# Another order of work in a local attention, and a quarter of a scan's product handed to GpSimd

## The chip, the cores and the metric

One NeuronCore of one Trainium2 chip runs the whole program. Its engines each run their own queue of instructions in order: TensorE (PE, with its weight loads as PEld), VectorE (DVE), ScalarE (ACT), GpSimd (POOL), and SyncE (SP), which here only issues DMAs. They meet through semaphores. The metric is device time in microseconds; a kernel's time is the median of its runs.

## The reference, cut to what matters

The reference is a stack of blocks on a residual of 4 sequences x 1024 tokens x 128 features in float32. The change touches two of them. The first is the selective scan, used once with 64 channels and 32 states and once with 256 channels and 16 states:

```python
def step(h, inputs):
    u_t, d_t, b_t, c_t = inputs
    dA = jnp.exp(d_t[..., None] * A)
    h = dA * h + (d_t * u_t)[..., None] * b_t[:, None, :]
    y = jnp.einsum('bdn,bn->bd', h, c_t)
    return (h, y)
```

The second is local attention with 8 heads of 64 features and windows of 64 tokens, each looking at its own window and the one before; it runs in four layers (two stages of depth 2):

```python
h = shift_token(x); qkv = h @ wqkv; q, k, v = jnp.split(qkv, 3, axis=-1)
q = l2norm(q) * qs; k = l2norm(k) * ksc
q, k = rotary_xpos(q, k)
sim = jnp.einsum('bhwid,bhwjd->bhwij', bq, bk)          # bq is q times 8, bk: own window and the one before
sim = jnp.where(mask, -jnp.finfo(sim.dtype).max, sim)
out = jnp.einsum('bhwij,bhwjd->bhwid', jax.nn.softmax(sim, axis=-1), bv)
x = x + out.reshape(b, n, INNER) @ wo
```

## The kernel before

The program is eight stages, one after the other. Within a stage each engine has its own hand-written order of calls inside a `Block`; a call begins with its waits and ends with the increment of a semaphore. `s.at(n)` is the value after n increments, so `pe.wait_ge(q_in.sem, q_in.at(i + 1))` waits for the copy of Q of tile i.

**The scan** (`scan`) takes 16 steps j for each run of one sequence (and half of the channels): 4 runs in stage 1 and 8 in stage 7, 192 steps. A step covers 128 partitions x 1024 time columns. ScalarE makes the decay in PSUM (L233), GpSimd the input product (L249) from rows of B that SP fetched, VectorE the scan (L258), TensorE spreads C over the partitions (`spread_c`, L207, PSUM banks 2 and 3, a single buffer), VectorE multiplies state by C (L273), and TensorE folds the product into banks 6 and 7 (L221). At the end of a run VectorE takes the sum (`take`, L264).

**Local attention** (`local_attention`) takes 32 tiles of 128 tokens in a layer, software-pipelined by `in_steps`: 4 tiles written out, a loop over groups of 4, the last tiles written out. The names, with their lines in the trace:

- SP: `fetch(i + 4)` brings the token-shifted input of a tile to its place with four DMAs (L1605 to L1608); `pair_values(i + 1)` waits for V of the tile (L1612) and copies its halves with two DMAs (L1614, L1615). In each step SP does `fetch(i + 4)`, then `pair_values(i + 1)`.
- TensorE: `scores` (L1674), `values` (L1691), `output` (L1708), `project_qk` (L1640), `project_v` (L1645), `turn_probs` (L1681), `turn_qk` (L1652), `masks` (L1660), `turn_in` (L1634), `turn_out` (L1700), in this order in a step.
- ScalarE: `exponential` (L1775), `square` (L1757), `copy_probs` (L1780), `copy_k` (L1770, L1771), `take_v` (L1764), `copy_out` (L1785), `copy_h` (L1752).
- VectorE: `maximum` (L1845), `subtract` (L1851), `normal` (L1857, L1860), `add` (L1866), `squares` (L1836), `rotate` (L1827, then L1829 and L1830), `copy_q` (L1841).
- GpSimd: `norm`, four instructions a tile (L1902, L1904, L1907, L1911).

`turn_in` and `output` share bank 7; `turn_qk`, `values` and `turn_out` share banks 5 and 6; scores, mask and turned probabilities share banks 3 and 4.

Of the kernel before, what the change touches and what calls it, by code (L numbers as in the profile page):

```python
# [14 lines left out]
P = 128  # L15
# [130 lines left out]
def scan(k, batches, halves_n, delta, du, parts, rows, stored, sel, a_col, fold, diag, u, out, gate, spare):  # L146
# [4 lines left out]
    c_up, decay_up, input_up, scanned, weighted, summed, y_taken = [  # L151
        k.count("scan_" + n) for n in ("c_up", "decay_up", "input_up", "scanned", "weighted", "summed", "y_taken")]
    lane_in = [k.count(f"scan_lane_in{s}") for s in range(U)]
    credited = (input_up, scanned, weighted, summed, y_taken)
    for s in credited:
        s.passed(U)
    runs = [(b, hf) for b in range(batches) for hf in range(halves_n)]
    with ExitStack() as mem:
        b_lane = k.arena[4].rearrange("p (s t) -> p s t", t=SEQ)
        ring2 = k.arena6.rearrange("p (r s t) -> p r s t", r=3, t=SEQ)  # L160
        inputs, weight = ring2[:, 0], ring2[:, 2]
        state = [ring2[:, 1, 0], ring2[:, 1, 1]] + spare
        bank = k.bank
        pieces = len(rows(0, 0))
        block = mem.enter_context(nc.Block())
# [7 lines left out]
        def ahead(o, j, n):  # L173

            if isinstance(j, int) and j + n >= J:
                return (o + 1, j + n - J) if o + 1 < len(runs) else None
            return o, j + n

        def steps(eng, body, begin=None):

            for o in range(len(runs)):
                if begin:
                    begin(o)
                with eng.Fori(0, J // U - 2) as jj:
                    for s in range(U):
                        body(o, jj * U + s, s)
                for j in range(J - 2 * U, J):
                    body(o, j, j % U)
# [13 lines left out]
        @block.tensor  # L202
        def _(pe):
            def spread_c(o, j):
                pe.wait_ge(weighted.sem, weighted.at(o * J + j))
                for c in range(2):
                    mm = pe.matmul(bank[2 + c], sel(j), parts(runs[o][0], c), start=True, stop=True)  # L207
                mm.then_inc(c_up.sem, 1)

            def begin(o):  # L210
                b, hf = runs[o]
                pe.wait_ge(y_taken.sem, y_taken.at(o))
                for c in range(2):
                    pe.matmul(bank[6 + c][0:M, :], diag(hf), u(b, hf, c), start=True, stop=False, skip_group_check=True)

            def body(o, j, s):
                pe.wait_ge(weighted.sem, weighted.at(o * J + j + 1))
                if ahead(o, j, 1):
                    spread_c(*ahead(o, j, 1))
                for c in range(2):  # L220
                    mm = pe.matmul(bank[6 + c][0:M, :], fold, weight[:, s % 2, c * BANK:(c + 1) * BANK], start=False,  # L221
                                   stop=isinstance(j, int) and j == J - 1, skip_group_check=True)
                mm.then_inc(summed.sem, 1)

            spread_c(0, 0)
            steps(pe, body, begin)

        @block.scalar
        def _(act):
            def decay_of(o, j, s):  # L230
                b, hf = runs[o]
                act.wait_ge(scanned.sem, scanned.at(o * J + j - 1))
                act.activation(decay(s), delta(b, hf), ACT.Exp, scale=a_col(hf, j)).then_inc(decay_up.sem, 1)  # L233

            def body(o, j, s):
                if ahead(o, j, 2):
                    decay_of(*ahead(o, j, 2), s)

            for j in range(2):
                decay_of(0, j, j)  # L240
            steps(act, body)

        @block.gpsimd
        def _(pool):
            def body(o, j, s):
                i = o * J + j
                pool.wait_ge(lane_in[s % U].sem, lane_in[s % U].at((i - s % U + U) * (16 * pieces // U)))
                pool.wait_ge(scanned.sem, scanned.at(i - 1))
                pool.tensor_tensor(inputs[:, s % 2], b_lane[:, s % U], du(*runs[o]), ALU.mult).then_inc(input_up.sem, 1)  # L249
            steps(pool, body)  # L250

        @block.vector
        def _(dve):
            def scan_step(o, j, s):
                i = o * J + j
                dve.wait_ge(decay_up.sem, decay_up.at(i + 1))
                dve.wait_ge(input_up.sem, input_up.at(i + 1))
                dve.tensor_tensor_scan(state[s % U], decay(s), inputs[:, s % 2], 0.0, ALU.mult, ALU.add).then_inc(  # L258
                    scanned.sem, 1)

            def take(o):
                b, hf = runs[o]
                dve.wait_ge(summed.sem, summed.at((o + 1) * J))
                dve.tensor_tensor(out(b, hf), two(6)[0:M, :], gate(b, hf), ALU.mult).then_inc(y_taken.sem, 1)  # L264

            def body(o, j, s):
                i = o * J + j
                if ahead(o, j, 1):
                    scan_step(*ahead(o, j, 1), s + 1)
                dve.wait_ge(scanned.sem, scanned.at(i + 1))  # L270
                dve.wait_ge(c_up.sem, c_up.at(i + 1))
                dve.wait_ge(summed.sem, summed.at(i - 1))
                dve.tensor_tensor(weight[:, s % 2], state[s % U], two(2), ALU.mult).then_inc(weighted.sem, 1)  # L273

            scan_step(0, 0, 0)
            steps(dve, body, lambda o: take(o - 1) if o else None)
            take(len(runs) - 1)

    n = len(runs)
    for s in (c_up, decay_up, input_up, scanned, weighted, summed):  # L280
        s.passed(n * J)
    y_taken.passed(n)
    for s in lane_in:
# [1222 lines left out]
def local_attention(k, depth):  # L1506
# [89 lines left out]
    with nc.Block() as block:  # L1596
# [32 lines left out]
        def _(pe):  # L1629
# [90 lines left out]
            def step(i, s4, ahead, before):  # L1720
                s = s4 % 2
                scores(i, s)
                if before:
                    values(i - 1, 1 - s)
                if before > 1:
                    output(i - 2, i + 4 if ahead > 3 else TILES)
                if ahead > 2:
                    project_qk(i + 3, (s4 + 3) % RING)
                if ahead:
                    project_v(i + 1, (s4 + 1) % RING)  # L1730
                turn_probs(i, s)
                if ahead:
                    turn_qk(i + 1, (s4 + 1) % RING)
                    masks(i + 1)
                if ahead > 3:
                    turn_in(i + 4, s4, i - 1 if before > 1 else 0)
                if before:
                    turn_out(i - 1, ahead)

            def finish(i, s4):  # L1740
                values(i, s4 % 2)
# [6 lines left out]
        def _(act):  # L1748
# [14 lines left out]
                    act.wait_ge(vb_in[1 - s].sem, vb_in[1 - s].at((i - 1 - (1 - s) + 2) * 16))  # L1763
                act.copy(VA[:, s, :, 0:HD], bank[2].rearrange("p (h d) -> p h d", d=HD)).then_inc(v_in.sem, 1)  # L1764

            def copy_k(i, s):
                act.wait_ge(t_up.sem, t_up.at(i + 1))
                act.wait_ge(s_up.sem, s_up.at(i))
                keys = bank[6].rearrange("p (c t) -> p c t", t=P)
                act.copy(KT[:, s, :, 0:P], keys)  # L1770
                act.copy(KT[:, 1 - s, :, P:KEYS], keys[:, :, WIN:P]).then_inc(k_in.sem, 1)  # L1771
# [15 lines left out]
            for i in range(RING):  # L1787
# [2 lines left out]
                    square(i, i % 2)  # L1790
                if i == 0:
                    take_v(0, 0)
            copy_k(0, 0)

            def step(i, s4, ahead, before):
                s = s4 % 2
                exponential(i, s)
                if ahead > 2:
                    square(i + 3, 1 - s)
                copy_probs(i)  # L1800
                if ahead:
                    copy_k(i + 1, 1 - s)
                    take_v(i + 1, 1 - s)
                if before:
                    copy_out(i - 1)
                if ahead > 3:
                    copy_h(i + 4, s4)
            in_steps(act, step, lambda i, s4: copy_out(i))

        @block.vector  # L1810
        def _(dve):
# [20 lines left out]
            def squares(i, s4):  # L1832
# [1 line left out]
                if not (isinstance(i, int) and i < RING):  # L1834
                    dve.wait_ge(rn_in.sem, rn_in.at(2 * (i - RING) + 1))
                dve.tensor_reduce(SS[:, s4, :], SQ[:, s4 % 2].rearrange("p (h d) -> p h d", d=HD), AX_X, ALU.add).then_inc(ss_in.sem, 1)  # L1836

            def copy_q(i, s):
                dve.wait_ge(t_up.sem, t_up.at(i + 1))
                dve.wait_ge(s_up.sem, s_up.at(i - 1))  # L1840
                dve.tensor_copy(QT[:, s].rearrange("p c t -> p (c t)"), bank[5]).then_inc(q_in.sem, 1)  # L1841

            def maximum(i, s):
                dve.wait_ge(s_up.sem, s_up.at(i + 1))
# [23 lines left out]
            for i in range(3):  # L1868
# [1 line left out]
                    squares(i, i)  # L1870
                rotate(i, i, 0)
                rotate(i, i, 1)
            copy_q(0, 0)

            def step(i, s4, ahead, before):
                s = s4 % 2
                maximum(i, s)
                subtract(i, s)
                if before:
                    normal(i - 1, 1 - s)  # L1880
                if before > 1:
                    add(i - 2)
                if ahead > 1:
                    squares(i + 2, (s4 + 2) % RING)
                if ahead > 2:
                    rotate(i + 3, (s4 + 3) % RING, 0)
                if ahead:
                    copy_q(i + 1, 1 - s)
                if ahead > 2:
                    rotate(i + 3, (s4 + 3) % RING, 1)  # L1890

            def finish(i, s4):
                normal(i, s4 % 2)
                add(i - 1)
                add(i)
            in_steps(dve, step, finish)
# [941 lines left out]
```

## Time and profile before

| | us |
|---|---|
| median of 3 runs | 3891.34 |
| lowest and highest | 3886.89, 3895.9 |
| the profiled execution | 3895.95 |
| its span, first to last instruction | 3893.4 |
| busy in the span: TensorE, VectorE | 2985.4, 2724.8 |
| busy in the span: GpSimd, ScalarE | 1742.9, 1552.9 |
| stage 1 scan, VectorE's scans | 156 to 378 |
| stage 7 scan, VectorE's scans | 2485 to 3021 |

Busy shares are means over stages with different limits, so the two edited stretches are read on their own. A timeline row gives start, duration, engine, line, operation, output and inputs, shape and count; the bracket holds the engine's idle time just before it and what ended it.

### The profile page before, as it was taken

What the parts mean: (1) busy time and instruction counts of PE and PEld (TensorE: products, weight loads), DVE (VectorE), ACT (ScalarE), POOL (GpSimd) and SP (SyncE); (2) the same over time, 40 slices, a digit from 0 to 9 for tenths busy, and PEclk for the clock granted to TensorE, in tenths of its full rate; (3) what the DMA queues carried; (4) which work ended last, traced back from release to release, by engine and by line L of the source; (5) the groups of instructions that cost most, each with busy time, mean ns of one, the idle gap of its engine ahead of it and who ended that gap; (6) DMA issues with size and microseconds to landing.
All of it is one profiled execution on the core that took longest, in us unless ns stands there. A gap on an engine that the chain in (4) does not pass through costs nothing. (4 is left out here: it accounts for less than half of the span.)

```text
span 3893.4 us, 65456 instructions
## 1 busy us (share of the span) xinstructions
PE 2985.4 (77%) x22063; PEld 1733.9 (45%) x22143; DVE 2724.8 (70%) x4138; ACT 1552.9 (40%) x2219; POOL 1742.9 (45%) x1111
## 2 busy tenths in 40 slices
PE   3677465659988994999889983667666599879987
PEld 1112354523434442666556662223222366646765
DVE  4699546447766763887478855698699688648874
ACT  3532123124444553555245532432433255425542
POOL 4465121131111102886078813465366488428861
PEclk8699678669999997999999996899899799989999
DMA  3354000032111200111011100242143111101110
GB/s 83 91 147 111 7 6 7 1 92 39 34 32 28 39 15 22 35 36 33 1 31 37 37 6 4 99 146 102 65 147 135 29 37 38 22 7 39 37 29 22
DMA packets 141586, 187.95 MB, mean 48 GB/s; under 512 B 74218, under 2 KB 88641, under 8 KB 141121
## 3 DMA queue, kind: packets, MB, share of 16 engines
q1 hardware_dynamic: 141388, 185.41, 18.0%
q8 instruction: 113, 1.85, 0.2%
q14 instruction: 85, 0.69, 0.1%
HBM read 132.76 MB, written 9.18 MB: 36 GB/s over the span
## 5 line engine op out<-in xcount | busy, mean ns | idle before, releaser
L249 POOL TENSOR_TENSOR arena<-arena 128x1024 f32<-128x1024 f32 x192 | 451.2, 2351 | 232.9 <-DVE arena L258 178.2
L1425 DVE TENSOR_REDUCE causal_peak_parts<-psum 128x1 f32<-128x512 f32 (+3 forms) x608 | 385.3, 661 | 142.1 <-PE psum L1300 77.1
L1904 POOL TENSOR_TENSOR arena<-arena,w_minus_half 128x16 f32<-128x16 f32 x128 | 372.8, 2912 | 175.8 <-DVE arena L1836 175.8
L1408 ACT ACTIVATE arena<-psum 128x1024 f32<-128x1024 f32 (+3 forms) x352 | 294.3, 870 | 342.4 <-PE psum L1331 165.7
L233 ACT ACTIVATE psum<-arena,w_A 128x1024 f32<-128x1024 f32 x192 | 214.4, 1118 | 460.7 <-DVE arena L258 387.8
L258 DVE TENSOR_TENSOR_SCAN arena<-psum,arena 128x1024 f32<-128x1024 f32 x160 | 364.5, 2279 | 28.5 <-POOL arena L249 28.5
L1902 POOL TENSOR_TENSOR arena<-arena 128x1024 f32<-128x1024 f32 x128 | 301.9, 2359 | 103.4 <-DVE arena L1830 103.4
L207 PE MATMUL psum<-arena,m_sel 96*128 96x512 bf16 x384 | 117.7, 389 | 229.4 <-DVE arena L273 202.1
L1640 PE MATMUL psum<-w_layer_wqkv,arena 128*128 128x512 f32 x512 | 266.1, 646 | 33.9 <-DVE arena L1830 32.5
L1775 ACT ACTIVATE arena<-arena 128x1024 f32<-128x1024 f32 x128 | 135.3, 1057 | 375.1 <-DVE arena L1851 375.1
L1297 PE MATMUL psum<-arena 128*128 128x512 bf16 (+3 forms) x746 | 229.3, 347 | 45.0 <-PEq L1033 25.1
L1911 POOL TENSOR_TENSOR arena<-arena 128x1024 f32<-128x1024 f32 x128 | 243.7, 1904 | 13.2 <-POOL arena L1907 5.3
L221 PE MATMUL psum<-arena,w_ident 128*128 128x512 f32 x512 | 244.1, 599 | 0.0
L1845 DVE TENSOR_REDUCE arena<-psum 128x8 f32<-128x1024 f32 x128 | 156.8, 1225 | 102.2 <-PE psum L1674 102.2
L1331 PE MATMUL psum<-arena 128*128 128x512 bf16 (+3 forms) x714 | 192.8, 327 | 31.5 <-ACT arena L1408 22.0
L1827 DVE TENSOR_TENSOR arena<-psum,arena 128x1024 f32<-128x1024 f32 x128 | 156.6, 1224 | 72.9 <-ACT arena L1757 72.6
L207 PEld LDWEIGHTS psum<-arena,m_sel 96*128 (+1 forms) x384 | 23.7, 97 | 391.0 <-issue 198.5
L1836 DVE TENSOR_REDUCE arena<-arena 128x16 f32<-128x1024 f32 x128 | 155.1, 1211 | 59.1 <-ACT arena L1757 59.1
L273 DVE TENSOR_TENSOR arena<-arena,psum 128x1024 f32<-128x1024 f32 x160 | 190.7, 1192 | 1.9 <-PE psum L207 1.7
L2037 PE MATMUL psum<-arena,w_layer_w 128*128 128x512 f32 (+1 forms) x384 | 179.8, 596 | 0.0
L1757 ACT ACTIVATE arena<-psum 128x1024 f32<-128x1024 f32 x128 | 131.1, 1024 | 104.0 <-PE psum L1640 104.0
L1780 ACT COPY arena<-psum 128x1024 f32<-128x1024 f32 x128 | 129.7, 1013 | 90.2 <-PE psum L1681 90.2
(338 smaller groups left out, 6594.8 us busy)
## 6 DMA issues: line engine op xcount, KB each, us to landing
arena<-scan_rows_large SPq DMA_DIRECT2D x128, 512.0 KB, 3.7
arena<-arena SPq DMA_DIRECT2D x256, 130.0 KB, 2.3
arena<-scan_rows_small SPq DMA_DIRECT2D x128, 256.0 KB, 3.8
arena<-causal_parts SPq DMA_DIRECT2D x288, 64.0 KB
causal_parts<-arena SPq DMA_DIRECT2D x8, 768.0 KB, 3.8
arena<-Z SPq DMA_DIRECT2D x128, 32.0 KB, 1.8
arena<-Z SPq DMA_DIRECT2D x128, 28.0 KB, 1.8
X<-in_L_attn_a_x SPq DMA_DIRECT2D x4, 512.0 KB, 6.2
```

Of the source, the lines that this page charges most:

```text
L221: mm = pe.matmul(bank[6 + c][0:M, :], fold, weight[:, s % 2, c * BANK:(c + 1) * BANK], start=False, stop=isinstance(j, int) and j == J - 1 ...
L233: act.activation(decay(s), delta(b, hf), ACT.Exp, scale=a_col(hf, j)).then_inc(decay_up.sem, 1)
L249: pool.tensor_tensor(inputs[:, s % 2], b_lane[:, s % U], du(*runs[o]), ALU.mult).then_inc(input_up.sem, 1)
L258: dve.tensor_tensor_scan(state[s % U], decay(s), inputs[:, s % 2], 0.0, ALU.mult, ALU.add).then_inc(scanned.sem, 1)
L1297: mm = pe.matmul(o, QK[:, s, 0, col + qt * P:col + (qt + 1) * P], QK[:, s, 1, col + half * BANK:col + half * BANK + size], start=True, sto ...
L1331: mm = pe.matmul(bank[bk][:, lo:hi], keys, QK[:, s, 0, q:q + hi - lo], start=True, stop=True)
L1408: act.activation(into, place, ACT.Exp, scale=SCALE).then_inc(probs.sem, 1)
L1425: dve.tensor_reduce(part[:, heads[0]:heads[0] + len(heads), qt, half:half + 1].rearrange("p h a -> p (h a)"), place[:, 0:len(heads) * size ...
L1640: mm = pe.matmul(bank[m], HT[:, s4, :], w["wqkv"][:, m * INNER:(m + 1) * INNER], start=True, stop=True)
L1902: pool.tensor_tensor(COS[s4], COS[s4], SIN[s4], ALU.add).then_inc(ready2.sem, 1)
L1904: pool.tensor_tensor(RN[:, s4, :], SS[:, s4, :], k.minus_half[:, 0:2 * HEADS], ALU.pow).then_inc(rn_in.sem, 1)
L1911: pool.tensor_tensor(heads, heads, RN[:, s4, :].unsqueeze(2).broadcast_to([P, 2 * HEADS, HD]), ALU.mult).then_inc(rot.sem, 1)
```

## The change

In the scan ScalarE copies the last 256 columns of the spread C into a tile of its own (two buffers), and GpSimd multiplies the last 256 columns of the state by it; VectorE multiplies the first 768. GpSimd's queue is written two steps ahead: the input product of step j+2, then the rest of step j. In local attention TensorE's `output` moves from ahead of the projections to behind `turn_qk`, `turn_in` from the end to ahead of `turn_probs`, `masks` to the end; `copy_q` moves from VectorE to ScalarE, ahead of K; `copy_h` comes ahead of `copy_probs`; VectorE's `add` comes one tile later.

```diff
-    credited = (input_up, scanned, weighted, summed, y_taken)
+    c_kept, weighted_rest = k.count("scan_c_kept"), k.count("scan_weighted_rest")
+    credited = (input_up, scanned, weighted, weighted_rest, c_kept, summed, y_taken)
+    MAIN = 3 * SEQ // 4
...
+        c_rest = mem.enter_context(nc.sbuf_tensor(k.name("scan_c_rest"), [P, 2, SEQ - MAIN], F32))
...
                 if ahead(o, j, 1):
                     spread_c(*ahead(o, j, 1))
+                pe.wait_ge(weighted_rest.sem, weighted_rest.at(o * J + j + 1))
...
+            def keep_c(o, j, s):
+                act.wait_ge(c_up.sem, c_up.at(o * J + j + 1))
+                act.wait_ge(weighted_rest.sem, weighted_rest.at(o * J + j - 1))
+                act.copy(c_rest[:, s % 2], two(2)[:, MAIN:SEQ]).then_inc(c_kept.sem, 1)
...
                     decay_of(*ahead(o, j, 2), s)
+                keep_c(o, j, s)
...
+            def weigh_rest(o, j, s):
+                i = o * J + j
+                pool.wait_ge(scanned.sem, scanned.at(i + 1))
+                pool.wait_ge(c_kept.sem, c_kept.at(i + 1))
+                pool.wait_ge(summed.sem, summed.at(i - 1))
+                pool.tensor_tensor(weight[:, s % 2, MAIN:SEQ], state[s % U][:, MAIN:SEQ], c_rest[:, s % 2], ALU.mult).then_inc(
+                    weighted_rest.sem, 1)
...
+            def body(o, j, s):
+                if ahead(o, j, 2):
+                    product(*ahead(o, j, 2), s + 2)
+                weigh_rest(o, j, s)
...
-                dve.wait_ge(c_up.sem, c_up.at(i + 1))
+                dve.wait_ge(c_kept.sem, c_kept.at(i + 1))
                 dve.wait_ge(summed.sem, summed.at(i - 1))
-                dve.tensor_tensor(weight[:, s % 2], state[s % U], two(2), ALU.mult).then_inc(weighted.sem, 1)
+                dve.tensor_tensor(weight[:, s % 2, 0:MAIN], state[s % U][:, 0:MAIN], two(2)[:, 0:MAIN], ALU.mult).then_inc(
+                    weighted.sem, 1)
...
                 if before:
                     values(i - 1, 1 - s)
-                if before > 1:
-                    output(i - 2, i + 4 if ahead > 3 else TILES)
                 if ahead > 2:
                     project_qk(i + 3, (s4 + 3) % RING)
                 if ahead:
                     project_v(i + 1, (s4 + 1) % RING)
+                if ahead > 3:
+                    turn_in(i + 4, s4, i - 2 if before > 2 else 0)
                 turn_probs(i, s)
                 if ahead:
                     turn_qk(i + 1, (s4 + 1) % RING)
-                    masks(i + 1)
-                if ahead > 3:
-                    turn_in(i + 4, s4, i - 1 if before > 1 else 0)
+                if before > 1:
+                    output(i - 2, i + 5 if ahead > 3 else TILES)
                 if before:
                     turn_out(i - 1, ahead)
+                if ahead:
+                    masks(i + 1)
...
-            def copy_k(i, s):
+            def copy_qk(i, s):
                 act.wait_ge(t_up.sem, t_up.at(i + 1))
                 act.wait_ge(s_up.sem, s_up.at(i))
+                act.copy(QT[:, s].rearrange("p c t -> p (c t)"), bank[5]).then_inc(q_in.sem, 1)
...
                     square(i + 3, 1 - s)
+                if ahead > 3:
+                    copy_h(i + 4, s4)
                 copy_probs(i)
                 if ahead:
-                    copy_k(i + 1, 1 - s)
+                    copy_qk(i + 1, 1 - s)
                     take_v(i + 1, 1 - s)
                 if before:
                     copy_out(i - 1)
-                if ahead > 3:
-                    copy_h(i + 4, s4)
...
-                if before > 1:
-                    add(i - 2)
+                if before > 2:
+                    add(i - 3)
...
                     rotate(i + 3, (s4 + 3) % RING, 0)
-                if ahead:
-                    copy_q(i + 1, 1 - s)
```

## Rows read from the trace of the kernel before

**Rows 1.** Busy time by stretch, steady local attention: PE, PEld, DVE, ACT, POOL, clock, DMA.

```profile
1599.00:1815.00 216.00, 208.32 (x2406) 150.29 (x2406) 182.94 (x240) 122.48 (x192) 174.59 (x96) 1.00 0.17 36
```

**Rows 2.** Timeline of TensorE, the scores that begin the step.

```profile
1740.77 1.10 PE L1674 MATMUL psum<-arena 64*64 64x128 f32 x32
```

**Rows 3.** Timeline of the same step, engines PE and ACT.

```profile
...
1742.88 1.16 PE L1708 MATMUL psum<-w_layer_wo,arena 128*128 128x128 f32 x8
...
1743.88 1.88 PE L1640 MATMUL psum<-w_layer_wqkv,arena 128*128 128x512 f32 x4
...
1744.54 1.06 ACT L1775 ACTIVATE arena<-arena 128x1024 f32<-128x1024 f32 x1 [2.92 <-DVE arena L1851]
...
1746.45 1.04 PE L1681 MATMUL psum<-w_ident,arena 128*128 128x128 f32 x8
...
1747.33 1.04 PE L1652 MATMUL psum<-w_ident,arena 128*128 128x128 f32 x8
1747.60 1.01 ACT L1780 COPY arena<-psum 128x1024 f32<-128x1024 f32 x1 [0.70 <-PE psum L1681]
...
1748.51 0.59 ACT L1770 COPY arena<-psum 128x512 f32<-128x512 f32 x1
...
1748.67 0.60 PE L1660 MATMUL psum<-arena,w_identb 128*128 128x512 bf16 x2 [0.30 <-ACT arena L1780]
...
1748.99 0.39 ACT L1771 COPY arena<-psum 128x256 f32<-128x256 f32 x1
...
1749.11 0.27 PE L1634 MATMUL psum<-w_ident,arena 128*128 128x128 f32 x1
...
1749.24 0.63 PE L1700 MATMUL psum<-w_ident,arena 128*128 128x128 f32 x4
1749.25 0.62 ACT L1764 COPY arena<-psum 128x512 f32<-128x512 f32 x1
...
1749.80 1.10 PE L1674 MATMUL psum<-arena 64*64 64x128 f32 x32
```

**Rows 4.** Timeline of SP: first and last DMA of two tiles.

```profile
...
1740.72 0.51 SPq L1614 DMA_DIRECT2D arena<-arena  x1
...
1745.16 0.56 SPq L1608 DMA_DIRECT2D arena<-Z  x1
1749.96 0.51 SPq L1614 DMA_DIRECT2D arena<-arena  x1
...
1753.82 0.54 SPq L1608 DMA_DIRECT2D arena<-Z  x1
```

**Rows 5.** Waits of SP from 1600 to 1815 us: total, times, longest.

```profile
SPq L1612 <- ACT arena L1764: 100.8, 24, 4.4
```

**Rows 6.** The line of the fourth fetch DMA (L1608), issue to landing.

```profile
DMA to landing us min/median/max: 1.6/1.7/2.4
```

**Rows 7.** Timeline of one steady step of the scan.

```profile
248.34 2.28 DVE L258 TENSOR_TENSOR_SCAN Z<-psum,arena 128x1024 f32<-128x1024 f32 x1
...
250.53 1.19 DVE L273 TENSOR_TENSOR arena<-Z,psum 128x1024 f32<-128x1024 f32 x1
250.65 1.12 ACT L233 ACTIVATE psum<-arena,w_A 128x1024 f32<-128x1024 f32 x1 [2.19 <-DVE Z L258]
250.75 2.35 POOL L249 TENSOR_TENSOR arena<-arena 128x1024 f32<-128x1024 f32 x1 [0.97 <-DVE Z L258]
251.65 2.27 DVE L258 TENSOR_TENSOR_SCAN arena<-psum,arena 128x1024 f32<-128x1024 f32 x1
...
251.87 0.59 PE L207 MATMUL psum<-arena,m_sel 96*128 96x512 bf16 x2 [0.86 <-DVE arena L273]
```

**Rows 8.** Groups of instructions by form: busy, mean ns, idle before.

```profile
L1079 POOL TENSOR_TENSOR arena<-arena 128x512 bf16<-128x512 f32 x16 | 18.4, 1157 | 20.8 <-ACT arena L1101 20.7
...
L1241 POOL TENSOR_TENSOR causal_low<-causal_low,causal_low_parts 32x128 f32<-32x128 f32 x16 | 6.7, 418 | 1.3
...
L1434 DVE TENSOR_TENSOR Z<-Z,psum 128x512 f32<-128x512 f32 x32 | 22.0, 688 | 34.3 <-PE psum L1309 34.3
```

More of the change, by code:

```diff
@@ L244, in _, with product @@
         def _(pool):
-            def body(o, j, s):
+            def weigh_rest(o, j, s):
[5 more added lines that the diff above has]
+                    weighted_rest.sem, 1)
+            def product(o, j, s):
                 i = o * J + j
@@ L249, in body @@
                 pool.tensor_tensor(inputs[:, s % 2], b_lane[:, s % U], du(*runs[o]), ALU.mult).then_inc(input_up.sem, 1)
+            def body(o, j, s):
+                if ahead(o, j, 2):
+                    product(*ahead(o, j, 2), s + 2)
+                weigh_rest(o, j, s)
+            for j in range(2):
+                product(0, j, j)
             steps(pool, body)
@@ L279, in scan @@
     n = len(runs)
-    for s in (c_up, decay_up, input_up, scanned, weighted, summed):
+    for s in (c_up, decay_up, input_up, scanned, weighted, weighted_rest, c_kept, summed):
         s.passed(n * J)
@@ L1792, in _ @@
                     take_v(0, 0)
-            copy_k(0, 0)
+            copy_qk(0, 0)
             def step(i, s4, ahead, before):
@@ L1836, in squares @@
                 dve.tensor_reduce(SS[:, s4, :], SQ[:, s4 % 2].rearrange("p (h d) -> p h d", d=HD), AX_X, ALU.add).then_inc(ss_in.sem, 1)
[L1838 to L1841, printed above, removed]
             def maximum(i, s):
@@ L1872, in _ @@
                 rotate(i, i, 1)
-            copy_q(0, 0)
             def step(i, s4, ahead, before):
@@ L1893, in finish @@
                 normal(i, s4 % 2)
+                add(i - 2)
                 add(i - 1)
```

## The prediction

> **What bounds the kernel now.** I read the two edited stretches one after the other: first the busy shares by stretch, then the timeline of one steady step, then the waits of SP. The stretches are regular: a step looks like its neighbour to within 0.3 us, so one step priced well and multiplied carries the forecast.
>
> In local attention a tile takes 9.0 us (216 us hold 24 tiles, 96 GpSimd instructions at four a tile) [rows 1]. TensorE is busy 208 of the 216 us at a granted clock of 1.00 (the upper of its two levels, 2.4 GHz), VectorE 183, GpSimd 175, ScalarE 122 [rows 1]. The reader should see that only TensorE has next to no room. The order of the step shows its one hole: `turn_qk` starts at 1747.33, eight transposes take about 0.88 us to issue (`turn_probs` at 1746.45, `turn_qk` at 1747.33), so `masks` could start near 1748.21 and starts at 1748.67, released by ScalarE's copy of the turned probabilities [rows 3]. That is 0.46 us in 9.03 (scores at 1740.77 and at 1749.80) [rows 2, 3]. The rest, 8.57 us, is work.
>
> What is not visible in busy shares is SP. It waits for ScalarE's copy of V in 24 of 24 tiles [rows 5]; then it issues the two copies of `pair_values`, then the four of `fetch`, and the last of these starts 4.44 us after the first `pair_values` (1740.72, 1745.16) or 3.86 (1749.96, 1753.82) [rows 4]. Of the four steps in a turn of the loop three take 3.86 to 3.98 and one 4.44: mean 4.04. That last fetch lands 1.7 us after its issue starts [rows 6]. Today nobody waits for it: counted from the scores, tile i+4's input is in at about 0.2 + 4.0 + 1.7 = 5.9 us, and `turn_in`, which wants it, runs at 8.34 (1749.11 minus 1740.77).
>
> In the scan VectorE is saturated: scan 2.28, product with C 1.19, starts 3.31 us apart [rows 7]. GpSimd's product takes 2.35 of that and ScalarE's decay 1.12 [rows 7].
>
> **The scan half.** 192 steps lose a quarter of the columns on VectorE. 1024 columns cost 1.19, 512 of a like instruction 0.69 [rows 7, 8]: 256 columns are worth 0.25 from that pair, 0.30 by plain proportion; I take 0.267, between the two. 192 x 0.267 = 51 us, if VectorE stays the bound at 3.05.
>
> Is it? ScalarE copies the last 256 columns of C. C is ready when two matmuls are through at 252.46, 0.8 us after the scan starts; a copy of 256 columns takes 0.39 [rows 3, 7]; it is there by about 253.0, a good 0.9 us before VectorE can ask at the end of the scan (253.9). ScalarE's decay started at 250.65 and is long over. Hidden; if it were not, the 0.39 would fall on VectorE each step (75 us).
>
> GpSimd gets 256 columns of product. Nearest rows: 0.42 for 128 columns on 32 partitions, 1.16 for 512 columns into bf16 [rows 8]; a line through them gives 0.67, a line from 0.42 to the 2.35 for 1024 columns 0.70. I take 0.70. GpSimd then has 2.35 + 0.70 = 3.05 and its hand-overs, 3.05 to 3.2 us against VectorE's 3.05. A small deficit does no harm: the product of step j+2 is wanted only at the start of scan j+2, some 1.3 us after it is done, and the fold of step j, which waits for the rest, comes behind `spread_c` with about the same slack. 15 steps at 0.1 us too much use up 1.3, and at each of the 12 run ends VectorE waits for the last fold anyway, so GpSimd catches up. Loss 0 to 11 us. Bounds: with 0.42 nothing is lost; with 1.16 GpSimd needs 3.5 us a step, more than today, and the half loses about 25 us instead of gaining. I take minus 50 us.
>
> The Trainium skill (GPSIMD Engine Reference, Engine selection) advises VectorE for elementwise work and calls GpSimd about twice as slow for two inputs. The pair here agrees, 2.35 against 1.19 for 1024 columns [rows 7]; by it the quarter moved costs GpSimd some 0.6 and the sum stays as it is.
>
> **The attention half, TensorE alone.** Removing the hole leaves 8.57. `turn_in` and `output` change places in the order; TensorE executes the same instructions. `turn_probs` waits for the exponential, which ends at 4.83 (1744.54 + 1.06 - 1740.77) [rows 2, 3]; scores, values, `project_qk`, `project_v` and `turn_in` fill 4.81 (5.68 from the scores to `turn_probs`, less 1.00 for `output`, plus 0.13 for `turn_in`) [rows 2, 3]. After that come 0.88 + 0.88 + 1.00 + 0.56 + 0.44 us for the two turns, `output`, `turn_out` and `masks`, so scores at about 8.7. The copy of Q moves from VectorE to ScalarE ahead of K: 0.48 us more in ScalarE's chain (spacing of a 512-column copy, 1748.51 to 1748.99) [rows 3]; K is then ready at about 8.5. On this path alone a step takes 8.75.
>
> **The attention half, through SP.** This is the step that decides. `turn_in(i+4)` moves from the end of step i to ahead of `turn_probs(i)`. Nothing in SP's queue moves: `fetch(i+4)` still stands behind `pair_values(i)`, which waits for `take_v(i)` at the end of ScalarE's step i-1. So a loop closes that was open: copy of V, SP's six issues, landing, `turn_in`, `turn_probs`, copy of the probabilities, copies of Q and K, next copy of V. Its length:
> - copy of V ends 1749.87, `pair_values` starts 1749.96: 0.09 [rows 3, 4]
> - to the last fetch: 4.04 [rows 4]
> - landing: 1.70 [rows 6]
> - `turn_in` to `turn_probs`: 0.13 seen between `turn_in` and the next group [rows 3], 0.15 taken
> - `turn_probs` to the copy of the probabilities: 1.15 (1746.45 to 1747.60) [rows 3]
> - that copy's start to the end of the copy of V: 2.27 (1747.60 to 1749.87) [rows 3], plus 0.48 for Q: 2.75.
>
> The sum is 9.88 us, against 8.75 for TensorE and 9.03 now. It binds. Queued behind TensorE's wait in `turn_in` are all of `turn_probs`, `turn_qk`, `output`, `turn_out`, `masks` and the next scores, and VectorE's maximum and ScalarE's exponential wait for those. `turn_in` would start at 6.0 us of the step, not 4.8. GpSimd (7.3 us a tile) and VectorE (7.6, less the copy of Q) stay covered [rows 1].
>
> 27 of the 32 tiles are on this loop (28 tiles call `turn_in`; the first one's fetch is issued in the prologue). 27 x (9.88 - 9.03) = 23 us a layer. To this come, as my estimates: the later phase of `turn_in`, paid once (6.0 - 4.8, 1.1); the last tiles, which call no `turn_in` and now have `output` between the turn of Q and K and the next scores (0.5 net); a slower first turn of SP's loop (1 to 2); and, as a gain, the first copy of Q, which no longer stands behind VectorE's rotations (up to 1). 25 us a layer, four layers: plus 100 us.
>
> The Trainium skill (DMA: Bandwidth & Descriptors, Rules for kernel authors) says to issue a DMA early and wait on its semaphore late; this edit waits earlier and issues no earlier, so the rule speaks against it. The same page of the Trainium skill (section Anatomy of one DMA) puts the fixed cost near 2.0 us; with that estimate in place of the measured landing the loop would be 10.2 us and the attention half some 130 us.
>
> **Sum.** The profiled execution took 3895.95 us (span 3893.4), 4.6 above the median of 3891.34. 3896 + 100 - 50 = 3946; against the median 3941, which I forecast.
>
> **Rivals.**
> - The transfer is hidden anyway (the other side). If input i+4 is in by 4.8 us of the step, the stated gain arrives: 0.28 us x 27 x 4 and the ends give about minus 35, with the scan minus 85: 3806. Against it: the loop would have to be a full microsecond shorter than its six terms. The sign turns at a loop of about 9.45 us: below it the attention half costs less than the scan's 50. For it: landings and issues overlap in ways that a sum of medians may overstate. Chance 0.10; a loop between 9.4 and 9.5, within 0.2% of before, 0.04.
> - GpSimd becomes the scan's bound: it takes 3.3 us or more a step and the scan gains nothing. For it: no row has 256 columns of float32, and three waits stand ahead of the new instruction. Then 3990, with the 1.16 bound 4015. Chance 0.08.
> - The loop is longer than summed: dynamic waits on SP, TensorE and ScalarE at the turn of each loop now all lie on it. 10.1 us gives another 24: 3965. This is a part of the forecast's own range.
>
> **How the numbers follow.** The forecast (loop binds, scan gains 40 to 54) has chance 0.78 and its own range 3912 to 3972: loop 9.65 to 10.1, and the scan's spread. Faster side 0.10, in between 0.04, GpSimd bound 0.08. The range 3905 to 3975 leaves out both rivals' cores. 0.2% (8 us) is what this kernel's runs can tell from no change: faster 0.11, same 0.05, slower 0.84.
>
> **What would show it.** After: scores of neighbouring tiles 9.8 to 10.0 us apart in all four layers; TensorE idle about 1.1 us a tile ahead of `turn_in`, released by the fetch DMA; no wait of `masks`; ScalarE's copy of the probabilities still waiting for TensorE. In the scan: starts 3.05 us apart, VectorE's product 0.92 us, GpSimd's new one near 0.70 with GpSimd busy nearly all of the time, run ends as long as before. Wrong if: steps of 8.7 to 9.0 (loop open), scan starts above 3.2 (GpSimd bound), or a wait of VectorE on ScalarE's copy of C.

## The result, and the profile after

| | us |
|---|---|
| before, median of 4 runs | 3893.62 (3886.89 to 3897.08) |
| after, median of 4 runs | 3956.09 (3937.97 to 3965.07) |
| ratio, after to before | 1.0161, 95% interval 1.0141 to 1.0181 |
| the profiled execution after | 3961.65, span 3959.5 |

The change makes the kernel 1.6% slower, about 63 us. Forecast were 50 us (3941) with a range of 3905 to 3975.

**Local attention after.** The view of busy time by stretch, steady tiles of the first layer, to be held against [rows 1] (PE, PEld, DVE, ACT, POOL, clock, DMA):

```profile
1700.00:1838.00 138.00, 122.75 (x1410) 87.33 (x1410) 97.82 (x128) 76.30 (x124) 101.77 (x56) 1.00 0.16 34
```

56 GpSimd instructions are 14 tiles in 138 us, 9.86 us a tile. TensorE, busy 96% of [rows 1], is busy 89%: the most loaded engine has become idler, and no other has become busier. That points to a chain through several engines, not to one engine at its limit. The clock is 1.00 as before. The timeline of one tile (answers to [rows 3]; L1701 scores, L1661 `turn_in`, L1708 `turn_probs`, L1809 the copy of the probabilities, L1797 Q, L1799 and L1800 K, L1792 V):

```profile
1736.73 0.63 ACT L1792 COPY arena<-psum 128x512 f32<-128x512 f32 x1
...
1737.24 1.10 PE L1701 MATMUL psum<-arena 64*64 64x128 f32 x32
...
1737.45 0.51 SPq L1641 DMA_DIRECT2D arena<-arena  x1
...
1741.02 1.06 ACT L1804 ACTIVATE arena<-arena 128x1024 f32<-128x1024 f32 x1 [3.16 <-DVE arena L1875]
...
1741.89 0.56 SPq L1635 DMA_DIRECT2D arena<-Z  x1
...
1743.73 0.32 PE L1661 MATMUL psum<-w_ident,arena 128*128 128x128 f32 x1 [1.54 <-DMA arena<-Z]
...
1743.89 1.04 PE L1708 MATMUL psum<-w_ident,arena 128*128 128x128 f32 x8
...
1745.04 1.01 ACT L1809 COPY arena<-psum 128x1024 f32<-128x1024 f32 x1 [0.68 <-PE psum L1708]
...
1745.95 0.59 ACT L1797 COPY arena<-psum 128x512 f32<-128x512 f32 x1
...
1747.17 0.63 ACT L1792 COPY arena<-psum 128x512 f32<-128x512 f32 x1
...
1747.67 0.56 PE L1701 MATMUL psum<-arena 64*64 64x128 f32 x12
```

The loop can be read off: V is copied at 1737.36, SP starts its six issues 0.09 later, the last one at 1741.89 (4.44, the long turn of SP's loop), `turn_in` starts 1.84 after that, `turn_probs` 0.16, the copy of the probabilities 1.15, the end of the next copy of V 2.76. From one end of V's copy to the next (1747.80) that is 10.44 us. Each link waits for the one before it, or stands behind it in its engine's order, and the last leads back to the first: that makes it a loop. The exponential was over at 1742.08, so TensorE stood for the DMA alone. The turn shown is the longest of the four in a turn of SP's loop; the three beside it take 9.67 to 9.69, and the mean is 9.87. The groups by line give the whole program's total; idle time before the group and its releaser stand behind the bar:

```profile
L1661 PE MATMUL psum<-w_ident,arena 128*128 128x128 f32 x128 | 42.5, 332 | 186.2 <-DMA arena<-Z 186.1
```

That is 111 waits. Four of them, 68 us in all, stand at the starts of the layers and were there before, where the line (L1634) had no others; the 107 new ones take 118 us, 1.10 each. The stretch of 32 tiles, from the first to the last `subtract`, grew from 277.4, 277.4, 277.2 and 277.3 us to 302.7, 304.3, 302.8 and 302.5: 103 us in four layers.

**The scan after** (timeline, answers to [rows 7]; L260 is GpSimd's new product, L242 ScalarE's copy of C):

```profile
250.02 0.92 DVE L299 TENSOR_TENSOR arena<-arena,psum 128x768 f32<-128x768 f32 x1
...
250.24 2.35 POOL L267 TENSOR_TENSOR arena<-arena 128x1024 f32<-128x1024 f32 x1
250.87 2.27 DVE L284 TENSOR_TENSOR_SCAN Z<-psum,arena 128x1024 f32<-128x1024 f32 x1
...
251.72 0.37 ACT L242 COPY scan_c_rest<-psum 128x256 f32<-128x256 f32 x1 [0.47 <-PE psum L210]
...
252.55 0.73 POOL L260 TENSOR_TENSOR arena<-arena,scan_c_rest 128x256 f32<-128x256 f32 x1
253.07 0.92 DVE L299 TENSOR_TENSOR arena<-arena,psum 128x768 f32<-128x768 f32 x1
...
253.29 2.35 POOL L267 TENSOR_TENSOR arena<-arena 128x1024 f32<-128x1024 f32 x1
253.91 2.27 DVE L284 TENSOR_TENSOR_SCAN Z<-psum,arena 128x1024 f32<-128x1024 f32 x1
```

Scans start 3.04 apart (250.87, 253.91) where they started 3.31 apart. GpSimd's two instructions begin 2.31 and 0.74 apart and fill the step; VectorE still sets it. Stage 1's scans from first to last start fell from 219.2 to 203.1 us.

### The profile page after: what moved, and what is told of

It reads as the page before. It is cut to its first block and busy times, and to the rows that moved or that the text cites. A ratio compares the mean times of both kernels' runs of the same rounds, so it can differ in the third digit from the quotient of the medians.

```text
span 3959.5 us, 66247 instructions
## 1 busy us (share of the span) xinstructions
PE 3005.1 (76%) x22063; PEld 1744.9 (44%) x22143; DVE 2585.9 (65%) x4010; ACT 1674.0 (42%) x2539; POOL 1870.4 (47%) x1303
## 5 line engine op out<-in xcount | busy, mean ns | idle before, releaser
L1661 PE MATMUL psum<-w_ident,arena 128*128 128x128 f32 x128 | 42.5, 332 | 186.2 <-DMA arena<-Z 186.1
L1809 ACT COPY arena<-psum 128x1024 f32<-128x1024 f32 x128 | 129.7, 1013 | 84.6 <-PE psum L1708 84.1
L1372 PE MATMUL psum<-arena,Z 128*32 128x512 f32 (+3 forms) x1536 | 163.5, 501 | 0.5 <-issue 0.3
```

## The experiments

Each kernel was timed in five rounds. The kernels of one batch share their runs of the kernel before: 3892.22 for e1 to e4, 3889.51 for e5 to e8, 3896.18 for e9 and e10, 3890.89 for e11. "Tile" is the mean distance of `subtract` over tiles 16 to 27, the four layers alike within 0.04 unless said.

**e1, the scan half alone.** `scan` from the changed kernel, `local_attention` from the one before.

> The scan half alone, local attention as before. My sum: 192 scan steps of 3.05 us in place of 3.31, so 51 us less than the kernel before (about 3843), and local attention's tiles 9.03 us apart again. Rival, that the two halves disturb each other (clock, SBUF or queues): the saving here differs from 51 by more than 8 us.

3848.05 us, ratio 0.9884 (0.9865 to 0.9903), 44 to 45 us less; tile 9.07. 51 us would be a ratio of 0.9869, just inside the interval. In the trace the two scans are shorter by 15.7 us (219.2 to 203.5, stage 1) and 32.7 us (533.7 to 501.0, stage 7), first to last start: 48 of the 51 us.

**e2, the attention half alone.**

> The attention half alone, the scan as before. My theory: about 100 us from the loop through SP and V (27 tiles of 9.87 in place of 9.03, four layers), and some 15 more from the lower clock after each layer: 3893 + 115 = 4008. If the 13 us that the whole change costs beyond my sum come from somewhere else than attention, this one gives 3993 or less.

4009.92 us, ratio 1.0303 (1.0279 to 1.0326): 118 us, tile 9.89 to 9.96. The two halves' effects, minus 45 and plus 118, add up to 73 against the 63 of the whole, inside the three intervals together (about 8 us each). Of the expected parts the second failed here: in its profile no long stretch at low clock follows a layer; the layers themselves took 302.7 to 307.3 us, 110 more in all, in part because their first twelve tiles were longer, and the ends of the layers added 5.

**e3, the fetch ahead of the copy of V's halves.** The changed kernel, only SP's order differs:

```diff
             for i in range(RING):
                 fetch(i, i)
-            pair_values(0, 0)
...
                 if ahead > 3:
                     fetch(i + 4, s4)
-                if ahead:
-                    pair_values(i + 1, (s4 + 1) % 2)
+                pair_values(i, s4 % 2)
```

> Both halves, but SP issues fetch(i+5) ahead of pair_values(i+1), so a tile's input no longer stands behind the copy of V of the step before. Every other engine's order is as in the changed kernel. Loop theory: turn_in no longer waits for a DMA, tiles 8.7 to 8.8 us apart, about 120 us less than the changed kernel, near 3810 to 3830. Rival, that turn_in ahead of turn_probs costs in itself (its wait for VectorE's add, ScalarE's longer chain): tiles stay above 9.3 and the time above 3890.

3821.48 us, ratio 0.9821 (0.9802 to 0.984); tile 8.70. The tile's wait is gone (what `turn_in` still waits for the DMA lies at the starts of the layers, as in the kernel before) and with it 1.17 us a tile. Busy time by stretch in e3:

```profile
1620.00:1794.00 174.00, 172.44 (x2018) 125.17 (x2017) 138.64 (x180) 106.43 (x179) 146.69 (x81) 1.00 0.17 37
```

TensorE is busy 172.4 of 174 us: now an engine binds. This run carries the verdict: with every other queue unchanged, the place of four DMA issues in SP's order is worth 135 us (3956 to 3821), more than the whole loss.

**e4, the copy of Q back on VectorE**, in the changed kernel: `copy_q` restored between the two parts of `rotate`, ScalarE's `act.copy(QT...)` taken out.

> The changed kernel with the copy of Q back on VectorE. Loop theory: that copy is 0.48 us of the loop of 9.87, so tiles come 9.39 apart, 27 x 4 x 0.48 = 52 us less than the changed kernel (about 3904). Rival, that TensorE's or ScalarE's load sets the step and not the loop: the tile moves by less than 0.2 us.

3911.87 us, ratio 1.0054 (1.0035 to 1.0073), 44 us less than the changed kernel; tile 9.38 to 9.41. The loop shrinks by the 0.48 us of the one copy, on an engine that is busy 55% of the time.

**e5, SP's new order in the kernel before**, the edit of e3 and nothing else.

> The kernel before with nothing changed but SP's order: fetch(i+5) ahead of pair_values(i+1), as in e3. My theory: in the kernel before the input lands 2.5 us before turn_in wants it, so SP's order is worth nothing there: tiles 9.07 apart, time within 0.2% of before (3885 to 3900). Rival, that the earlier fetch is worth something in itself (a freer SP or DMA queue) and e3 owes part of its 71 us to it: 10 us or more faster than before.

3889.91 us, ratio 0.9998 (0.9985 to 1.0011); tile 9.07. The fetch was early enough before; the order is worth something only once `turn_in` asks early.

**e6, V copied first on ScalarE**, in the changed kernel:

```diff
                 if ahead:
-                    copy_qk(i + 1, 1 - s)
                     take_v(i + 1, 1 - s)
+                    copy_qk(i + 1, 1 - s)
```

> The changed kernel with V copied ahead of Q and K on ScalarE; SP's order as in the changed kernel. Loop theory: Q (0.48) and K's two copies (0.48, 0.26) leave the loop, 9.88 - 1.22 = 8.66, so the path through K binds instead: the copy of V (about 0.5) now lies ahead of K's, scores at 8.9 to 9.0. Tiles 8.9 to 9.1 apart, 3850 to 3870. Rival (only the DMA's landing and not the copy of V decides): tiles stay near 9.87.

3868.06 us, ratio 0.9942 (0.9925 to 0.996); tile 9.20. The loop lost its 1.22 us and another path took over, as expected, but not the one named. Two rows of e6's timeline (L1797 the copy of Q, L1727 `turn_out`):

```profile
1703.81 0.60 ACT L1797 COPY arena<-psum 128x512 f32<-128x512 f32 x1
...
1704.56 0.63 PE L1727 MATMUL psum<-w_ident,arena 128*128 128x128 f32 x4 [0.41 <-ACT arena L1797]
```

`turn_out` writes the bank that Q is copied from, waits for that copy, and `masks` and the scores stand behind it on TensorE: 0.1 to 0.3 us more than my path through K.

**e7, 320 columns on GpSimd** in place of 256, `MAIN = 11 * SEQ // 16` in the changed kernel. This looks for the point at which GpSimd becomes the scan's bound.

> The changed kernel with 320 columns on GpSimd in place of 256. GpSimd needs 2.35 + 0.89 = 3.24 us a step (0.731 for 256 columns, 2.3 ns a column more) and VectorE 2.98. If GpSimd's 3.08 was already close to the bound, GpSimd now sets the step: starts 3.2 to 3.25 apart once the slack of 1.3 us is used, about 15 to 30 us slower than the changed kernel. If GpSimd had room, the step falls to 2.98 and the kernel gains 12 us.

3954.96 us against 3956.09 for the changed kernel: no difference, neither of the two sizes. The trace shows why: within each run of 16 steps both hold, one after the other. In stage 1's second run the scans start 2.98 us apart nine times, then 3.04 to 3.14. GpSimd's cycle in the later steps (timeline; L260 with 320 columns):

```profile
239.26 0.87 POOL L260 TENSOR_TENSOR arena<-arena,scan_c_rest 128x320 f32<-128x320 f32 x1
...
240.09 2.36 POOL L267 TENSOR_TENSOR arena<-arena 128x1024 f32<-128x1024 f32 x1
...
242.40 0.87 POOL L260 TENSOR_TENSOR arena<-arena,scan_c_rest 128x320 f32<-128x320 f32 x1
```

The cycle is 3.14 us (239.26 to 242.40) against VectorE's 2.98. A deficit of 0.15 us a step is borne for nine steps, 1.4 us, and then GpSimd sets the pace. That is close to the slack of 1.3 us worked out in the prediction. The two scans together are 5 us longer than in the changed kernel's trace (204.0 and 504.6 against 203.1 and 500.7), so 320 columns are no better than 256.

**e8, `output` ahead of `turn_probs` in the last four tiles**, on e3.

```diff
+                elif before > 1:
+                    output(i - 2, TILES)
                 turn_probs(i, s)
...
-                if before > 1:
-                    output(i - 2, i + 5 if ahead > 3 else TILES)
+                if ahead > 3 and before > 1:
+                    output(i - 2, i + 5)
```

> e3 with the old place of output (ahead of turn_probs) in the last four tiles of a layer, where no turn_in is called. TensorE then works while the exponential runs. The last three tiles go from 8.56 to 8.2 to 8.4 us apart (1 us a layer), and if the idle stretch of 2.6 us ahead of turn_probs is what drops the clock behind a layer (24 us at 1.2 GHz in e3, 3 to 7 before), some 4 us more in two or three layers: 8 to 16 us less than e3, near 3810. If the clock drop has another cause: 3 to 4 us less.

3832.82 us, 11 us more than e3: a miss. The last three tiles are 9.46 us apart, not 8.2. `output` of tile i-2 waits for VectorE's `add` of tile i-3, and that now comes after `normal` of the same step, about when the exponential ends. Two rows of e8's timeline (L1890 `add`, L1733 `output`); the view gives `output` no releaser, but it starts 0.10 behind the end of that `add`:

```profile
1810.58 0.28 DVE L1890 TENSOR_TENSOR Z<-Z,psum 128x128 f32<-128x128 f32 x1
...
1810.96 1.13 PE L1733 MATMUL psum<-w_layer_wo,arena 128*128 128x128 f32 x8 [1.55 <-issue]
```

TensorE stands 1.55 us and then has `output`'s 0.97 ahead of `turn_probs` besides. The later `add` is part of the new order, and `output` can't be moved back without it.

**e9, the last four tiles in the order of before, `add` included**, on e3: for `ahead <= 3` `output(i - 2)` ahead of `project_qk`, `masks` behind `turn_qk`, `add(i - 2)`; tile 28 does `add(i - 3)` as well.

> e3 with the last four tiles of a layer in the order of the kernel before, VectorE's add included (e8 had left the add one tile late, and output waited for it). The last two tiles fall from 8.56 to 8.2 to 8.45; the first of the four is longer (output waits once for an add). By busy time alone 0 to 3 us less than e3. If the clock drop behind a layer comes from the idle stretch ahead of the last turn_probs (2.6 us in e3, 1.5 before), the low-clock stretch there returns to 3 to 7 us in all layers and e9 comes out 5 to 12 us below e3; if not, 24 us stretches remain in some layers.

3820.84 us, the same as e3: a miss, 5 to 12 less were expected. The last two tiles are 8.28 apart, but the one of transition takes 11.8 to 14.8: its `output` waits for an `add` and VectorE's second `add` for that `output`. TensorE stands 2.6 us there in all four layers. The clock held in one of them (11.8), was at the lower of its two levels, 1.2 GHz, for 3 us in two (13.1), and for 7 us in the first (14.8). The view of that one (columns as in [rows 1]):

```profile
1792.00:1799.00 7.00, 6.41 (x14) 3.75 (x15) 1.91 (x4) 1.46 (x2) 3.45 (x2) 0.51 0.01 2
```

No long stretch at 1.2 GHz follows any layer. Against e3's trace the four layers are 16.5 us longer and their ends 21 us shorter; a stretch ahead of the first layer that no edit touches is 9 us longer in this execution, which is why the gain doesn't show.

**e10, e3 with the copy of Q on VectorE.**

> e3 with the copy of Q back on VectorE. TensorE is busy 172 of 174 us in e3, so a shorter chain on ScalarE is worth nothing in the steady tiles: 8.70 apart again, time within 0.2% of e3. Rival, that K's copy on ScalarE still holds the scores up: tiles fall to 8.6 or less (10 us faster); or VectorE now holds up turn_out: above 8.8.

3836.75 us, ratio 0.9846 (0.9829 to 0.9863), 15 us more than e3; tile 8.85. The second rival holds. In e10's timeline (L1867 VectorE's copy of Q, L1725 `turn_out`):

```profile
1702.73 0.68 DVE L1867 COPY arena<-psum 128x512 f32<-128x512 f32 x1
...
1703.56 0.63 PE L1725 MATMUL psum<-w_ident,arena 128*128 128x128 f32 x4
```

`turn_out` starts 1.11 us behind the start of `output` (1702.45), against 0.98 in e3 (1706.68, 1707.66), and 0.15 behind the end of VectorE's copy (1703.41). So the move of Q to ScalarE is worth 0.15 us a tile where the loop is open, and costs 0.48 where it is closed (e4).

**e11, e9 with a gentler transition**: tile 28 issues `output` behind `project_v` and does its second `add` last.

> e9 with a gentler change of order: tile 28 issues its output behind project_v and adds last on VectorE, so TensorE does not stand 2.6 us ahead of output. The interval behind tile 28 falls from 11.8 to 14.8 us to about 9.7, the last two stay 8.3, and no low-clock stretch of 24 us follows a layer: 12 to 18 us less than e3 and e9, near 3806. If the interval shrinks but 24 us stretches return, the idle gap is not what drops the clock.

3798.63 us, ratio 0.9759 (0.974 to 0.9778): 92 us less than before, 23 less than e3, the fastest kernel of the study. The interval behind tile 28 is 9.19, tile 8.70. The layers take 268.8 us as in e3; the difference lies at their ends (21 us between the two traces). The two views of the 26 us from the last `turn_probs` of the first layer on, e3's and then e11's:

```profile
1809.00:1835.00 26.00, 18.23 (x92) 14.67 (x91) 6.25 (x24) 4.24 (x5) 1.21 (x2) 0.54 0.00 1
```

```profile
1809.00:1835.00 26.00, 17.45 (x101) 11.85 (x102) 9.48 (x34) 7.38 (x10) 2.42 (x4) 0.93 0.00 1
```

The granted clock is 0.54 in the one and 0.93 in the other, and e11 is further on in its work (101 matmuls begun against 92).

## Why the prediction was right

By its own steps:

- **The loop through SP binds.** Right, and shown: the wait stands in the trace (118 us of TensorE ahead of `turn_in`, 1.10 a tile, released by the fetch; 1.1 were forecast), e3 removes it by SP's order alone, e5 shows that the order by itself is worth nothing, e4 and e6 shorten the loop at two other places and the tile follows. Length forecast 9.88, measured 9.87 to 9.90 (tiles 16 to 27). Landing to `turn_in` was 1.84 in the row above, not 1.70; a few other terms are shorter.
- **Attention plus 100 us.** 103 in the four layers, first to last `subtract`. The forecast's 9.03 for a tile before was one ordinary step, and the mean of four is 9.07; that makes 22 us a layer of its 23.
- **TensorE alone would take 8.75 a tile.** 8.70 in e3. The rival of the hidden transfer, priced at 3806, is what e3 builds; it came to 3821, for it inherits the costs at the ends of the layers.
- **The scan minus 50.** Minus 49 in the scans of the trace after (219.2 to 203.1, 533.7 to 500.7), minus 48 in e1's, with step 3.04 (3.05 forecast), VectorE's product 0.92, GpSimd's 0.73 (0.70 taken).
- **The slack of 1.3 us behind GpSimd.** 1.4 us in e7.
- **The sum.** 50 forecast, 63 measured between the medians and 66 between the two profiled executions. The 66 divide so: the layers plus 103, the ends of the layers plus 20, the scans minus 49, the rest minus 8. Of this rest some 3 us are the gain that the prediction put at up to 1 us a layer, the first copy of Q: from stage 7's last scan to the first `subtract` of the third layer it takes 70.9 to 71.5 us in the five kernels that copy Q on VectorE (before, e1, e4, e5, e10) and 67.8 to 70.2 in the eight others. The remaining 5 us are luck: they lie between stage 1's scan and the first layer, 1188.5 us before and 1182.5 after, in work that no edit touches. Over the traces that stretch goes from 1173 us, some 330 of it at 1.2 GHz by the granted clock, to 1192 with some 380. The term that was mis-sized is the ends of the layers, put at 0.5 us net each. The last three distances did cost only 0.25, but what comes behind them cost 5 a layer, and the forecast had no term for it. In the first layer of the trace after, the last `turn_probs` comes after 2.6 us of idle TensorE, and then 26 us run at a granted clock of 0.54, where before it was 0.87 in that place:

```profile
1847.00:1873.00 26.00, 18.24 (x91) 14.55 (x90) 6.49 (x26) 4.24 (x5) 1.22 (x2) 0.54 0.00 1
```

```profile
1844.00:1870.00 26.00, 17.91 (x101) 12.26 (x100) 9.55 (x32) 6.98 (x9) 2.42 (x4) 0.87 0.00 1
```

(the first is after, the second before). The other three layers after have the same 2.6 us and shorter stretches at the lower clock. From the last `subtract` of a layer to the first of the next, over the feed-forward, it is 138.5 and 137.2 us after, 133.6 and 133.1 before; from the second layer to stage 7's first scan 238.3 against 232.8; at the program's end 121.6 against 115.6. In e3 the first two are 138.4 each, in e11, whose last tiles do not have that idle stretch, 131.4 and 129.9.

These 20 us have two parts. From the last `subtract` to the next long idle stretch of TensorE (4.44 us, ahead of the feed-forward) every layer before takes 12.0 us. The order after takes 13.5 in e7's third layer, where the clock stayed at 1.00 throughout: 1.5 us is the price of the order itself. After it is 19.0, 14.9, 16.5 and 17.0: the rest goes with the lower clock. That the order of the last tiles brings the low clock the traces show by number: in the 32 layers with the 2.6 us of idle TensorE just there (after, e2, e3, e4, e6, e7, e8, e10) the clock fell within 9 us of the last `subtract` in 24, and stayed low for 17 us or more in 10; in the 20 without it (before, e1, e5, e9, e11) never. Whether the idle stretch or the thinner work behind it decides, and why 24 and not 32, stays open; e9, with the same 2.6 us amid dense work, had a short drop behind three of four. The spread of the runs decides nothing: it is 27 us for the changed kernel, 8 for e3 with two long stretches in its trace, and 23 for the kernel before in e3's batch.

## What to carry to other kernels

When a consumer is moved forward in one engine's order, follow what it waits for back to the queue that issues it, and look at what that queue stands behind: here four DMA issues stood behind a wait for the end of another engine's previous step, and an open chain became a loop through ScalarE, SP, a DMA and TensorE, longer than any engine's work. Such a loop shows as every engine growing idler at once; add up one turn of it from timeline rows before the edit, and let the producer move as far forward as the consumer. A small imbalance between two engines in a stage with regular pauses is free up to the slack between them, and a saving with a slightly late engine should be checked against the number of steps between pauses.

## What the runs showed of the hardware

- An idle stretch of TensorE of 2.6 us at the end of a layer, with thinner work behind it, was followed within 9 us by the lower clock in 24 of 32 layers, for 3 to 27 us, and in 8 not. Stretches of 1.5 us, two in the tiles before it, were not. The longest cost some 7 us: 138.4 us to the next layer in e3 against 131.1 in e2 and 131.5 in e7, which have the same last tiles and only 3 us at the lower clock.
- The Trainium skill (DMA: Bandwidth & Descriptors, Anatomy of one DMA) gives a fixed cost near 2.0 us for a DMA that GpSimd issues. Those here are issued by SP, and the trace is below that figure: the one of 0.2 KB landed 1.6 to 1.8 us after its issue began, and its reader started 1.84 us after. The bulk of the loop's DMA part was SP's issuing: 3.9 to 4.4 us for six small DMAs.
- On GpSimd a pair of float32 products of 1024 and 256 columns, 2.35 and 0.73 us by their rows, started every 3.05 us; the rows overlap slightly, and so the engine's cycle is a little under the sum of its rows (3.14 against 3.23 in e7).
